# A fused attention kernel over 32 images: each engine's image loop written out with constant counts

## What is computed

```python
x = _L0_conv_ref(x, ...)                 # group norm, q/k/v (1x1), softmax(q k^T / sqrt(128)) v, projection, + x
t = _to_tokens(x)                        # 1024 tokens of 128 channels
t = t + _L1_attn_ref(_ln_t(t), ...)      # 8 search heads of 16, 2 retrievers: softmax over 1024 keys,
                                         # then a softmax gate over the 2 retrieved values
t = t + _L1_ffn_ref(_ln_t(t), ...)       # two 128x128 weights, one of them decoded from 4-bit codes
x = _from_tokens(t, x)
```

```python
search_attn = jax.nn.softmax(jnp.einsum('bsid,bsjd->bsij', sq, sk), axis=-1)
retrieved   = jnp.einsum('bsij,brjd->bsird', search_attn, rv)
retrieval_attn = jax.nn.softmax(jnp.einsum('bsid,bsird->bsir', rq, rk), axis=-1)
out = jnp.einsum('bsir,bsird->bsid', retrieval_attn, retrieved)
```

## Time and profile before

| | us |
|---|---|
| median of 3 runs | 4804.96 (4800.92 to 4805.71) |
| the profiled execution, own time | 4802.95 |
| its span in the trace | 4801.1 |
| PE busy | 4608.7 (96%) |
| POOL busy | 4242.2 (88%) |
| DVE busy | 3906.7 (81%) |
| ACT busy | 3317.4 (69%) |

### The profile page before, as it was taken

One profiled execution on the slowest core, in us unless ns is written; L12 is line 12 of the kernel. 1 busy time (PEld: TensorE's weight loads), 2 busy tenths in 40 slices (PEclk: granted clock), 3 DMA queues, 4 the chain that ended last, 5 costly groups with the idle time before them and its releaser, 6 DMA issues.

```text
span 4801.1 us, 102107 instructions
## 1 busy us (share of the span) xinstructions
PE 4608.7 (96%) x29838; PEld 2533.9 (53%) x29838; DVE 3906.7 (81%) x8190; ACT 3317.4 (69%) x6657; POOL 4242.2 (88%) x1142
## 2 busy tenths in 40 slices
PE   5899999999999999999999999999999999999985
PEld 4555555555555555555555555555555555555532
DVE  4788888888888888888888888888888888888863
ACT  2567777777777777777767777767777777777654
POOL 1589999999999999999999999999999999999996
PEclk9899999999999999999999999999999999999987
DMA  1011111111111111111111111111111111111010
GB/s 33 23 45 45 50 32 45 32 45 45 49 32 45 32 45 45 49 32 45 32 45 45 49 32 45 32 45 46 49 32 46 31 45 49 45 32 49 24 40 14
DMA packets 92739, 191.77 MB, mean 40 GB/s; under 512 B 16744, under 2 KB 50920, under 8 KB 92400
## 3 DMA queue, kind: packets, MB, share of 16 engines
q1 hardware_dynamic: 92400, 186.45, 13.9%
HBM read 17.53 MB, written 16.78 MB: 7 GB/s over the span
## 4 chain that ended last, share of the span: by engine, by line
PE 85%; DVE 6%; ACT 4%; issue 3%; POOL 1%; SPq 0%; DVEq 0%; ACTq 0%; DMA 0%; POOLq 0%
PE ps_u L804 18%; PE ps_bank L769 13%; PE ps_bank L791 11%; PE ps_bank L755 10%; PE ps_bank L741 4%; PE ps_bank L679 4%; DVE max_part L1067 4%; PE ps_bank L690 3%; PE ps_bank L710 3%; ACT p L962 3%; PE ps_bank L813 3%; PE ps_bank L743 3%; PE ps_bank L744 2%; PE ps_bank L742 2%; DVE max_part L1051 2%
## 5 line engine op out<-in xcount | busy, mean ns | idle before, releaser
L645 POOL TENSOR_TENSOR p_sum<-p_sum,p 128x2048 f32<-128x2048 f32 x768 | 3510.8, 4571 | 363.6 <-ACT p L962 316.6
L1067 DVE TENSOR_REDUCE max_part<-ps_bank 128x1 f32<-128x512 f32 x4096 | 2570.5, 683 | 513.0 <-PE ps_bank L769 500.8
L962 ACT ACTIVATE p<-ps_bank 128x512 f32<-128x512 f32 x4096 | 2153.3, 612 | 564.4 <-PE ps_bank L791 553.4
L804 PE MATMUL ps_u<-p,rv 128*32 128x512 f32 x8192 | 996.8, 604 | 3.2 <-ACT u_sb L968 2.5
L769 PE MATMUL ps_bank<-k_stack,q_stack 63*128 63x512 f32 x4096 | 863.5, 451 | 65.4 <-DVE max_part L1067 17.7
L791 PE MATMUL ps_bank<-q_stack,k_stack 64*128 64x512 f32 x4096 | 839.8, 449 | 35.2 <-ACT p L962 20.2
L791 PEld LDWEIGHTS ps_bank<-q_stack,k_stack 64*128 64x128 f32 x4096 | 372.0, 186 | 518.9 <-ACT p L962 177.0
L645 POOL TENSOR_TENSOR p_sum<-p 128x2048 f32<-128x2048 f32 x128 | 584.1, 4563 | 69.3 <-ACT p L962 69.3
L769 PEld LDWEIGHTS ps_bank<-k_stack,q_stack 63*128 63x128 f32 x4096 | 372.4, 185 | 507.6 <-DVE max_part L1067 199.2
L755 PE MATMUL ps_bank<-v,p 128*128 128x129 f32 x4096 | 498.9, 277 | 2.6 <-ACT p L919 1.6
L755 PEld LDWEIGHTS ps_bank<-v,p 128*128 128x128 f32 x4096 | 471.9, 191 | 38.1 <-DVE t_front L1097 12.5
(11 more groups left out here) (139 smaller groups left out, 4475.8 us busy)
## 6 DMA issues: line engine op xcount, KB each, us to landing
k_stack<-k_hi SPq DMA_DIRECT2D x256, 128.0 KB, 2.6
q_stack<-q_hi SPq DMA_DIRECT2D x256, 128.0 KB, 2.8
x_sb<-in_x SPq DMA_DIRECT2D x32, 512.0 KB, 3.6
k_stack<-k_lo SPq DMA_DIRECT2D x128, 128.0 KB, 2.6
q_stack<-q_lo SPq DMA_DIRECT2D x128, 128.0 KB, 2.8
t_held<-t_front SPq DMA_DIRECT2D x32, 512.0 KB, 2.9
rqk<-tok_next SPq DMA_DIRECT2D x32, 512.0 KB, 3.6
t_core<-t_held SPq DMA_DIRECT2D x32, 512.0 KB, 3.9
```

The source lines that it names most:

```text
L645: pool.tensor_tensor(p_sum[:, phase % 2, :, :], before, p1[:, step % ring, :, :], ALU.add)\
L804: last = pe.matmul(ps_u[n * QUAD:(n + 1) * QUAD, :], rv[:, key_tile, :], p1[:, step % ring, n, :], start=(key_tile == 0), stop=(key_tile = ...
L962: act.activation(p1[:, step % ring, n, :], bank_of("scores", index // 2, n % 2), ACT.Exp, scale=scale1)\
L1067: dve.tensor_reduce(max_part1[:, phase % 2, i, n, half:half + 1], bank_of("max1", index // 2, side), AXIS.X, ALU.max)\
```

## The change

`in_order` writes out every turn with plain integers. The loop on each engine, its register arithmetic, the branch back and the hint for it are gone. Lists, banks, buffers, semaphores and the counts waited for stay as they are. Below `in_order` all line numbers are smaller by 15.

```diff
@@ in_order
     first = -min(ahead for _, _, ahead, _ in order)
     last = images - 1 - max(ahead for _, _, ahead, _ in order)
-    for b in range(last + 1 - images, first):
-        turn_of(b)
-    before = links.count if links else 0
-    turn_of(first)
-    per_turn = links.count - before if links else 0
-    with nc.Fori(first + 1, last + 1, engines=[engine.engine], hint_back_edge=True) as b:
-        if banks:
-            banks.image = Image(b, banks.image - first - 1, 0)
-        if links:
-            links.looped = (b - first - 1) * per_turn
-        turn_of(b)
-    if banks:
-        banks.image = last + banks.image.ahead
-    if links:
-        links.looped = (last - first - 1) * per_turn
-    for b in range(last + 1, first + images):
+    for b in range(last + 1 - images, first + images):
         turn_of(b)
```

## The result

The changed kernel takes 4818.11 us (median of 9 runs, 4816.58 to 4822.19) against 4804.96 us (median of 9, 4800.92 to 4809.5): ratio 1.0028, 95% interval 1.0018 to 1.0038. It is slower by 13 us, or 0.3%, with an interval clear of no change; 4821 us was forecast.

What follows compares the result with a forecast made beforehand. PE, busy 96% of the span, was taken to set the pace. Terms of -15.7 and +32.8 us gave +17.1 us on the profiled 4802.95 us, so 4820 us, put at 4821 us; range 4804 to 4834 us.

Steps and rivals of the forecast that it cites:

- The sum: Turns 2 to 29 written out: each takes turn 1's 144.48 us, against 4028.47 us in the loop, +17.0 us.
- the microsecond put on top: Whole time: the forecast was put one microsecond up from 4820 us, at 4821 us.
- Part 1, the back edge: PE at the loop's branch, seen at `turn_den`: without the branch 0.56 us a turn is gained, 15.7 us in all.
- Part 2, the form of the waits: PE's matmuls with two waits, as at `scores.29`: written out they start later, 1.17 us a turn, 32.8 us lost.
- The estimate of about 12 places at 0.1 us: PE's two-wait matmuls: about 12 places in a turn lose 0.1 us each; most others are hidden.
- the forecast's signs: Changed profile, if right: turns 1 to 29 take 144.3 to 144.6 us, with no "issue" idle time at `turn_den`.
- the first two rivals: Turn 1's excess does not recur: faster, 4787 us, chance 0.09; or recurs partly: no difference, 4801 to 4810 us, 0.11.
- the third: PE's straight code also meets missing instructions, one 0.56 us gap a turn: 15.7 us more, 4836 us, chance 0.04.
- The rule on unrolling: Trainium skill: a taken branch breaks instruction prefetch, one reason to unroll fully; alone it makes the change a pure gain.

Runs made afterwards that it cites:

- The two turned runs: PE's waits ahead of each instruction given in reverse order: in the written-out changed kernel 4791.46 us, in the kernel before with its loops 4829.03 us.

## Why the prediction was right

- **The sum.** 28 x 144.48 - 4028.47 = +17.0 us was forecast for the turns, and +17.0 us came. That the fit is this close is partly luck: it rests on one turn, and the changed kernel's own turns 1 to 29 take 144.38 to 144.83 us. The median moved by 13 us, and 4821 us was 3 us too high. One of them was the microsecond put on top; the rest lies at the ends of the profiled execution, 0.9 us more ahead of turn 2 and 2.6 us less from turn 30 on, which no term covered.
- **Part 1, the back edge, -15.7 us.** The gap at `turn_den` is gone in all turns, and the first pieces of the 28 turns gave 13.5 us back, 7.4 us with half the branches. Without the hint PE's branch itself took over 4 us, so the gap comes from the branch. The term was 2.2 us too large, because turn 2, from which it was taken, is also a little shorter than the loop's mean in its other pieces.
- **Part 2, the form of the waits, +32.8 us.** Direction and size held: the other three pieces cost 30.5 us. This term was too large by the same 2.3 us, for it was measured from turn 2 as well, so in the sum the two errors cancel. The reason was put one step short. The text said that in written-out code an instruction ahead wakes first, as if this came with constants. The runs show that it comes with the order: in the loop the last-named wait ended on the matmul, written out the first-named one did. The kernel names the wait for a bank's reader behind the one for the operand, and at `scores.29` the bank that ACT reads behind the one that DVE reads. The two turned runs move 0.88 and 0.95 us a turn, near the 1.17 us of the term. Turning PE leaves 2.9 of the 30.5 us in those pieces. The waits of ACT, DVE and POOL, which the prediction had counted inside turn 1 without a price of their own, are worth 0.19 to 0.30 us a turn when they are turned, but not as a loss against the loop: with PE alone written out the turn was as long. The estimate of about 12 places at 0.1 us was near: turning PE shortens 17, by 0.08 us each, and a part of that is lost again elsewhere.
- **Rivals.** Turn 1 was no odd sample: turns 1 to 29 all take 144.4 to 144.8 us (a few lie above the 144.6 us of the forecast's signs), so the first two rivals fall. Against the third, straight code showed no issue gap on PE in turns 2 to 29.
- **The rule on unrolling** had by itself given 4787 us. The cost of the branch that it speaks of is real, 13.5 us here, yet the change that follows it was slower, since the compiled waits changed with it.

## What to carry to other kernels

A change that leaves every matmul of the bound engine in place can still move it by which of two waits the matmul itself holds: the one released last belongs on the instruction, the other ahead of it. Before forecasting what unrolling does, look for turns that are already unrolled (a prologue, a first pass) and compare them with the loop's, matmul by matmul. Here unrolling together with the turned waits on four engines gained 0.5% where unrolling alone lost 0.3%.

## What was not expected of the hardware

A back edge with its hint still cost PE between nothing and about 0.9 us: the first pieces of turns 3 to 29, all entered by the branch, take 2.82 to 3.75 us against 2.83 us in written-out code. Without the hint it cost 3.6 us a turn more. A wait that is released last and stands ahead of a matmul instead of on it costs 0.08 to 0.1 us at a place where PE is waiting. Waits that are already satisfied cost nothing that can be seen: 1351 waiting instructions fewer on PE left the time at 4819 us.
